# An RNN step with h stationary in four column tiles, and its sums turned on VectorE

## What is computed

```python
x = x + L0(x, cond)                       # modulated product with a 512x512 weight
# L1
xW = einsum('ntd,dh->nth', x, Wx) + b
h = cond
for t in range(128):
    h = tanh(h @ Wh + xW[:, t])           # 32x512 by 512x512
x = x + h_t
x = x + L2(x, cond)                       # base product and a low-rank one per sequence
x = x + L3(x, cond)                       # an LSTM over the 128 steps, 512 to 4x512
```

## Time and profile before

| | |
|---|---|
| median of 3 runs | 1167.6 us (1166.99 to 1167.61) |
| span of the profiled execution | 1166.8 us |
| mean granted clock of TensorE | 0.993 |
| TensorE busy | 1130.2 us (97%), 23548 matmuls |
| VectorE busy | 899.6 us (77%), 2660 instructions |
| ScalarE busy | 424.4 us (36%) |
| RNN matmuls | 2048 of 64 columns, 2048 of 32 columns |

### The profile page before, as it was taken

How to read it: one execution, slowest core, us unless ns; L and a number is a source line. 1 busy time by engine, 2 the same in 40 slices (tenths; PEclk the granted TensorE clock), 3 DMA queues, 4 the chain that set the end, 5 groups by cost and what they waited for, 6 DMA issues and landing times.

```text
span 1166.8 us, 52111 instructions
## 1 busy us (share of the span) xinstructions
PE 1130.2 (97%) x23548; PEld 773.9 (66%) x23548; DVE 899.6 (77%) x2660; ACT 424.4 (36%) x1036; POOL 53.7 (5%) x75
## 2 busy tenths in 40 slices
PE   5879999999999999999999999999999999999997
PEld 3546766776676677667667766766776676677587
DVE  6898877777877777787777778777777777777665
ACT  6784333333333333333333333333333333333232
POOL 1000100000000000000000000000000000000000
PEclk9889999999999999999999999999999999999999
DMA  9991000000000000000000000000000000000000
GB/s 337 404 347 33 21 21 21 3 21 21 21 20 21 21 3 21 21 21 21 21 20 4 21 21 21 21 21 17 7 21 21 21 21 21 12 3 12 12 13 21
DMA packets 24590, 51.08 MB, mean 44 GB/s; under 512 B 4160, under 2 KB 4288, under 8 KB 23344
## 3 DMA queue, kind: packets, MB, share of 16 engines
q1 hardware_dynamic: 23936, 47.49, 11.5%
q10 hardware_dynamic: 432, 0.26, 0.1%
HBM read 39.36 MB, written 8.39 MB: 41 GB/s over the span
## 4 chain that ended last, share of the span: by engine, by line
PE 92%; DMA 3%; DVE 2%; SPq 1%; ACT 1%; issue 1%; ACTq 0%; DVEq 0%
PE ps_gates L1523 55%; PE ps_l L1459 14%; PE ps_x L1459 7%; PE ps_rnn L1569 6%; PE ps_rnn L1572 4%; DMA ring<-in_hw 2%; PE ps_lr L1459 2%; PE ps_z L1459 2%; PE ps_l L1523 2%; SPq L395 1%; PE ps_gates L1429 1%; DMA rows<-in_ln_b 1%; SPq L426 0%; DVE gates_ring L1094 0%; SPq L415 0%
## 5 line engine op out<-in xcount | busy, mean ns | idle before, releaser
L1523 PE MATMUL ps_gates<-big,lstm_h 128*32 128x512 f16 (+1 forms) x6144 | 344.6, 373 | 1.5 <-DVE lstm_h L1127 1.2
L1523 PE MATMUL ps_gates<-big,rows 128*32 128x512 f16 (+1 forms) x6144 | 343.5, 372 | 0.6 <-ACT rows L514 0.6
L1523 PEld LDWEIGHTS ps_gates<-big,rows 128*32 128x32 f16 x6144 | 168.1, 97 | 158.8 <-issue 2.3
L1523 PEld LDWEIGHTS ps_gates<-big,lstm_h 128*32 128x32 f16 x6144 | 158.2, 97 | 148.1 <-DVE lstm_h L1127 2.0
L650 ACT ACTIVATE gates_ring<-gates_ring 128x256 f32<-128x256 f32 x128 | 53.4, 417 | 333.1 <-DVE gates_ring L1094 333.1
L1094 DVE SCALAR_TENSOR_TENSOR gates_ring<-ps_gates,tile_un,rows 128x256 f32<-128x256 f32 x248 | 108.6, 477 | 73.9 <-PE ps_gates L1523 73.9
L1569 PE MATMUL ps_rnn<-rnn_h,wh_hi 128*128 128x64 f16 x2048 | 120.5, 192 | 2.0 <-DVE rnn_h L928 1.9
L1572 PE MATMUL ps_rnn<-rnn_h,wh_lo 128*128 128x32 f16 x2048 | 116.3, 177 | 0.0
L1569 PEld LDWEIGHTS ps_rnn<-rnn_h,wh_hi 128*128 128x128 f16 x2048 | 93.0, 96 | 34.7 <-issue 27.4
L1572 PEld LDWEIGHTS ps_rnn<-rnn_h,wh_lo 128*128 128x128 f16 x2048 | 91.1, 97 | 0.0
L1124 DVE SCALAR_TENSOR_TENSOR late<-gates_ring,tile_g,cell_tanh 128x128 f16<-128x128 f32 x127 | 44.6, 352 | 60.2 <-ACT cell_tanh L659 60.2
(11 more groups left out here) (199 smaller groups left out, 1605.2 us busy)
## 6 DMA issues: line engine op xcount, KB each, us to landing
ring<-in_hw SPq DMA_DIRECT2D x16, 1024.0 KB, 14.8
xT_sb<-in_xT SPq DMA_DIRECT2D x32, 256.0 KB, 2.9
outT<-late SPq DMA_DIRECT2D x32, 256.0 KB, 2.0
big<-in_wx SPq DMA_DIRECT2D x5, 1024.0 KB, 14.7
big<-in_wh SPq DMA_DIRECT2D x5, 1024.0 KB, 14.3
big<-in_w SPq DMA_DIRECT2D x1, 1024.0 KB, 6.0
big<-in_hw SPq DMA_DIRECT2D x1, 1024.0 KB, 13.3
late<-in_base SPq DMA_DIRECT2D x1, 1024.0 KB, 14.3
```

Of the source, the lines that this page charges most:

```text
L1523: last = nc.tensor.matmul(by_chunk_of_gate(bank[B * j:B * j + B, columns]), of_step, tile_columns(w, j)[:, gates], start=start, stop=stop, ...
```

## The change

The two halves of the RNN weight become the two halves of one buffer, `wh1_16`. On TensorE h is stationary in four column tiles, as in the LSTM. The high half of h meets both halves of the weight in one matmul of 256 columns (128 of the high weight, 128 of the low); there are 16 of these (four chunks by four column tiles), and they wait for `rnn_hi_ready`. Then 16 matmuls of 128 columns take the low half of h with the high weight, behind the wait for `rnn_lo_ready`. So a step keeps 32 matmuls, streams 6144 columns where it streamed 1536, and does so in four tiles. The result, 128 partitions by 256 columns (two parts by four chunks by 32), has the batch on the partitions; VectorE turns its 32x32 blocks in one transpose from PSUM into a new buffer `rnn_turned` (fp32), and the two sums read that. The high and low half of h in `rnn_h16` lie one behind the other. The order of the steps in every engine's list is not changed.

```diff
--- before.py
+++ after.py
@@ -52,7 +52,8 @@
 
         w0_hi, w0_lo = sb("w0_hi", [P, KC, D], fp16), sb("w0_lo", [P, KC, D], fp16)
         wx1_hi, wx1_lo = sb("wx1_hi", [P, KC, H], fp16), sb("wx1_lo", [P, KC, H], fp16)
-        wh1_hi, wh1_lo = sb("wh1_hi", [P, KC, H], fp16), sb("wh1_lo", [P, KC, H], fp16)
+        wh1_16 = sb("wh1_16", [P, 2, KC, H], fp16)
+        wh1_hi, wh1_lo = wh1_16[:, 0], wh1_16[:, 1]
         base_hi, base_lo = sb("base_hi", [P, KC, D], fp16), sb("base_lo", [P, KC, D], fp16)
         a_hi, a_lo = sb("a_hi", [P, 2, KC, P], fp16), sb("a_lo", [P, 2, KC, P], fp16)
         b_hi, b_lo = sb("b_hi", [P, 2, D], fp16), sb("b_lo", [P, 2, D], fp16)
@@ -157,10 +158,11 @@
         b3_sb = rows[:, 0]
         x3_16 = [rows[:, 1 + q].bitcast(fp16).rearrange("p (h k n) -> p h k n", h=2, k=KC) for q in range(2)]
         x3_lr = rows[:, 3]
+        rnn_turned = sb("rnn_turned", [P, 2, KC, B])
         rnn_half = sb("rnn_half", [P, KC, B])
         rnn_pre = sb("rnn_pre", [P, KC, B])
         newton = sb("newton", [P, KC, B])
-        rnn_h16 = sb("rnn_h16", [P, KC, 2, B], fp16)
+        rnn_h16 = sb("rnn_h16", [P, 2, KC, B], fp16)
         cell = sb("cell", [P, P])
         added = sb("added", [P, P])
         cell_tanh = sb("cell_tanh", [P, P])
@@ -272,6 +274,7 @@
         x3_hi_ready, x3_lo_ready = sem("x3_hi_ready"), sem("x3_lo_ready")
 
         rnn_ps = sem("rnn_ps")
+        rnn_turned_ready = sem("rnn_turned_ready")
         rnn_half_ready = sem("rnn_half_ready")
         rnn_pre_ready = sem("rnn_pre_ready")
         rnn_h_ready = sem("rnn_h_ready")
@@ -304,6 +307,9 @@
 
         def tile_columns(w, j):
             return w.rearrange("p (k g j q) -> p j g k q", k=KC, g=GATES, q=B)[:, j]
+
+        def hidden_columns(w, j):
+            return w.rearrange("p h (k j q) -> p j h k q", j=KC, q=B)[:, j]
 
         def by_gate(x):
             return x.rearrange("p (g k q) -> p g k q", g=GATES, q=B)
@@ -638,7 +644,7 @@
 
             def rnn_high(r):
                 act.wait_ge(rnn_h_ready, r + 1)
-                high(rnn_h16[:, :, 0], x2T[r // STEPS % X2_RING][:, :, r % STEPS], s_h).then_inc(rnn_hi_ready, 1)
+                high(rnn_h16[:, 0], x2T[r // STEPS % X2_RING][:, :, r % STEPS], s_h).then_inc(rnn_hi_ready, 1)
 
             def rnn(r):
                 rnn_tanh(r)
@@ -693,7 +699,7 @@
             act.wait_ge(ld_wh1, 16)
             unused_squares(big[:, WH1_SLOT], 3, 2)
             act.wait_ge(h_scale_ready, 1)
-            high(rnn_h16[:, :, 0], condT_sb[:], s_h).then_inc(h0_hi, 1)
+            high(rnn_h16[:, 0], condT_sb[:], s_h).then_inc(h0_hi, 1)
             wx1_high(1)
             act.wait_ge(u_ready, 1)
             nc.scalar.activation(hyperT, hyperT, ACT.Gelu).then_inc(hyper_ready, 1)
@@ -915,17 +921,19 @@
                 dve.wait_ge(rnn_ps, r + 1)
                 if s == 0:
                     dve.wait_ge(xw1_ready, i + 1)
-                sums = ps_rnn[:, 0:2 * P].rearrange("p (k h b) -> p k h b", h=2, b=B)
-                nc.vector.scalar_tensor_tensor(rnn_half[:], sums[:, :, 1], un_rnn[:], xw1T[:, :, s],
+                nc.vector.transpose(rnn_turned[:].rearrange("p h k b -> p (h k) b"), by_chunk(ps_rnn[:, 0:2 * P]))\
+                  .then_inc(rnn_turned_ready, 1)
+                dve.wait_ge(rnn_turned_ready, r + 1)
+                nc.vector.scalar_tensor_tensor(rnn_half[:], rnn_turned[:, 1], un_rnn[:], xw1T[:, :, s],
                                                ALU.mult, ALU.add).then_inc(rnn_half_ready, 1)
                 dve.wait_ge(rnn_half_ready, r + 1)
-                nc.vector.scalar_tensor_tensor(rnn_pre[:], sums[:, :, 0], un_rnn[:], rnn_half[:],
+                nc.vector.scalar_tensor_tensor(rnn_pre[:], rnn_turned[:, 0], un_rnn[:], rnn_half[:],
                                                ALU.mult, ALU.add).then_inc(rnn_pre_ready, 1)
 
             def rnn_out(r):
                 i, s = r // STEPS, r % STEPS
                 dve.wait_ge(rnn_hi_ready, r + 1)
-                nc.vector.scalar_tensor_tensor(rnn_h16[:, :, 1], x2T[i % X2_RING][:, :, s], s_h, rnn_h16[:, :, 0],
+                nc.vector.scalar_tensor_tensor(rnn_h16[:, 1], x2T[i % X2_RING][:, :, s], s_h, rnn_h16[:, 0],
                                                ALU.mult, ALU.subtract).then_inc(rnn_lo_ready, 1)
 
             def x2(i):
@@ -1205,7 +1213,7 @@
                                     hb1T_sb[:].unsqueeze(2).broadcast_to([P, KC, B]), ALU.add).then_inc(u_ready, 1)
             wx1_low(0)
             dve.wait_ge(h0_hi, 1)
-            low(rnn_h16[:, :, 1], condT_sb[:], s_h, rnn_h16[:, :, 0]).then_inc(h0_lo, 1)
+            low(rnn_h16[:, 1], condT_sb[:], s_h, rnn_h16[:, 0]).then_inc(h0_lo, 1)
             weight_scale(3, 4, wh1_scale_ready)
             dve.wait_ge(wh1_scale_ready, 1)
             linked(nc.vector.tensor_tensor(un_rnn[:], s_wh1, s_h, ALU.mult))
@@ -1562,15 +1570,18 @@
                     gates_h(t, (1,), ((0, 0), (0, 1), (1, 0)), True).then_inc(gates_ps, 1)
 
             def rnn(r):
+                wait(pe, rnn_hi_ready, r)
+                for k in range(KC):
+                    for j in range(KC):
+                        nc.tensor.matmul(ps_rnn[B * j:B * j + B, 0:2 * P].rearrange("p (h k q) -> p h k q", h=2, q=B),
+                                         rnn_h16[:, 0, k], hidden_columns(wh1_16[:, :, k], j), start=(k == 0), stop=False,
+                                         tile_position=(0, B * j))
                 wait(pe, rnn_lo_ready, r)
-                for oc in range(KC):
-                    at = 2 * B * oc
-                    for k in range(KC):
-                        nc.tensor.matmul(ps_rnn[:, at:at + 2 * B], wh1_hi[:, k, P * oc:P * oc + P],
-                                         rnn_h16[:, k].rearrange("p h b -> p (h b)"), start=(k == 0), stop=False)
-                    for k in range(KC):
-                        last = nc.tensor.matmul(ps_rnn[:, at:at + B], wh1_lo[:, k, P * oc:P * oc + P], rnn_h16[:, k, 0],
-                                                start=False, stop=(k == KC - 1))
+                for k in range(KC):
+                    for j in range(KC):
+                        last = nc.tensor.matmul(by_chunk(ps_rnn[B * j:B * j + B, 0:P]), rnn_h16[:, 1, k],
+                                                hidden_columns(wh1_16[:, 0:1, k], j)[:, 0], start=False,
+                                                stop=(k == KC - 1), tile_position=(0, B * j))
                 last.then_inc(rnn_ps, 1)
 
             pe.wait_ge(consts_ready, 2)
```

## The result

| | before | after |
|---|---|---|
| median | 1167.4 us (measured beside it) | 1171.9 us (1170.35 to 1175.08) |
| ratio | 1 | 1.0043 [1.003, 1.0055] |
| span of the profiled execution | 1166.8 us | 1169.2 us |
| RNN step on TensorE | 0.88 us | 0.67 us |
| one tile | 34.05 us (the loop's first 34.45) | 33.9 to 34.4 us (the loop's first two 35.4 and 34.9, its last 33.2), mean of the loop 34.16 |

A forecast was written before the change was run, and what follows sets the result against it. TensorE was taken to bound the long middle. From a span of 1166.8 us, -24.9 (TensorE), +2.9 (stall) and +0.5 (start) make -21.5; with 0.8 to the median, 1146.1 us, range 1140 to 1166.

The forecast's parts named there:

- its saving: TensorE's RNN step falls from 0.88 to 0.67 us: 0.86 a tile, 24.9 us over 29 tiles.
- The changes of tiling: TensorE's switches between full-array and column-tiled work: moved at no cost; two more a tile would be 5 us.
- the wait for the high half: TensorE's new wait for the high half of h before an RNN step: met early, adding no delay.
- Rivals 1 and 3: TensorE's floor holds for every matmul, 1163 to 1168 us, 17%; VectorE's transpose dear, 1183 at 0.80 us, 8%.
- rival 2: VectorE bound a little, collision staying or dearer transpose: 0.2 to 0.5 us more stall a tile, 1152 to 1161 us, 15%.
- what was booked: New TensorE stall at the high half of the LSTM's h: 0.1 us a tile, 2.9 us in all.
- I give back 0.4 us: On VectorE, x1's low half moves away from GpSimd's product and shortens, cutting the added time from +1.10 to +0.70.
- the sums are as long from SBUF: VectorE's RNN sums take 349 ns from SBUF against 351 from PSUM, so moving their operand costs nothing.
- the first thing that is late: The high half of the LSTM's h, which TensorE takes up 1.32 us after it is ready, comes out level.
- the prediction's own sum: At the LSTM's high half of h: 1.5 us to spare, less VectorE's 0.70 and TensorE's 0.86, gives -0.06.
- The start was booked at +0.5: Eight RNN steps before 100 us, where DMA and VectorE rule: +0.5 us, bounds -3 and +3.
- nothing in the trace goes below about 27.5 ns: Possible TensorE floor per matmul with weight load, the low part's upper bound: 0.44 us, where 0.23 was taken.

The follow-up runs named there:

- e1: The changed kernel without VectorE's transpose, the sums reading PSUM unturned, so its RNN values are not the reference's: 1143.57 us.
- e13: The changed kernel with the wait for the low half of h ahead of all matmuls of an RNN step: 1171.15 us.
- e2: The changed kernel with the transpose writing the free half of its own PSUM bank, where the two sums read it: 1151.18 us.
- e8: e2 with VectorE taking lstm_sums(t + 1) before rnn_sums(r + 1), and x1_low and rnn_out(r + 1) behind the LSTM step: 1162.33 us.
- e14: e8 with ScalarE's order turned as well, the LSTM gates of step t + 1 ahead of the RNN's tanh: 1145.21 us.
- e3: The changed kernel with GpSimd's product for L0 held back until VectorE's tile scales after the second LSTM step: 1160.28 us.
- e10: The changed kernel with the transpose made twice in each RNN step: 1218.72 us.

## Why the prediction was wrong

**What held.** The windows were read rightly for before: TensorE was the bound. The step on TensorE is 0.67 us and its saving 25.1 us for 24.9 (e1), of which 23.0 in the tiles that were counted. The changes of tiling cost 0.05 us a tile at most, and the wait for the high half nothing that can be told (e13). The transpose takes 0.44 us, with its link 0.48. Rivals 1 and 3 are out: 128 columns in four tiles go 0.055 us a group, and the transpose is far from 0.67 us. What came is rival 2's mechanism, VectorE as the bound with the collision staying, but larger: 0.85 us of stall a tile is 0.75 over what was booked, where the rival gave 0.2 to 0.5.

**What failed, by size.** The step "I give back 0.4 us". It followed the low half of x1 out of GpSimd's product, rightly (745 ns in the mean of the 32), and did not ask what moved in. GpSimd starts the product a nearly fixed time after it has spread the maximum of x (7.49 us before, 7.24 now), and VectorE's queue behind that maximum had become longer by the transposes; so the instruction beside it was now an RNN sum. That sum had read one tensor from PSUM, and the change itself gave it both from SBUF. The prediction even compared the two forms, 349 against 351 ns, and took this for "the sums are as long from SBUF"; that is true only while GpSimd is quiet. Instead of 0.4 us a tile given back, VectorE has 22.5 us of stretching where it had 16.5. e2 takes exactly this away, and 21.2 of the 27.5 us between e1 and the kernel after go with it.

**What failed, by place.** The prediction took the high half of the LSTM's h for the first thing that is late. 2.6 us ahead of it TensorE needs the PSUM bank. In the trace of before, VectorE's timeline has the instruction that frees it:

```profile
520.55 0.86 DVE L1094 SCALAR_TENSOR_TENSOR gates_ring<-ps_gates,tile_un,rows 128x256 f32<-128x256 f32 x2
```

The line has both halves of the bank's sums; the second ends at 521.41. TensorE was to take the bank up halfway through the 96 products of 519.73, at 519.73 + 2.60 = 522.33: 0.92 to spare, not 1.32. No wait showed there, so no view named it; the code's waits do. A tile with a mean collision (0.45 us for this tile's 0.83) has 1.30. By the prediction's own sum with its 0.4 given back, 1.30 - 0.70 - 0.86 = -0.26 us a tile; the measured stall with nothing stretched is 33.37 - 33.24 = 0.13 (e2). With the collision kept and grown to 22.5 / 32 = 0.70 us, VectorE's addition is 1.10 + 0.70 - 0.45 = 1.35, and 1.30 - 1.35 - 0.86 = -0.91; measured is 34.09 (the median tile) - 33.24 = 0.85. So the method carries, given the right point and the right duration, though this was worked out with the result in hand; the 0.1 us a tile that was booked had both wrong. One term of the sum is also wrong by its own rows: 1.32 to spare beside a collision of 1.57 is 1.32 + 1.57 - 1.17 = 1.72 beside a median one, not 1.5. With 1.72 the sum gives +0.16, no stall at all, so this slip lay on the side of the result and hid a little of the miss.

**Why the time came out as if nothing had been saved.** The path that now sets the tile runs from the bank through one `gates_x` (2.60 us), one LSTM step's products (2.89 until VectorE takes them up at 531.72) and then VectorE's queue from there to the end of the next `lstm_sums(t + 1)` (559.31 + 0.87 = 560.18, so 28.46). These make 33.95 us from 526.23 to 560.18; with the 0.05 until TensorE starts, that tile is 34.00. No RNN matmul is in them. TensorE's saving could not shorten it; that it came to within 0.1 us of the old tile, nothing in the two traces ties together.

**The rest.** The start was booked at +0.5: the first LSTM step of the loop begins at 99.73, where it began at 98.91, so +0.8. The first two tiles took 35.42 and 34.90 us (e1: 34.06 and 33.24), which the prediction had as ordinary ones. From the kernel e1 to the kernel after the spans differ by 27.5 us: 25.8 in the 29 tiles (990.60 against 964.78), 0.8 in the start and 0.8 behind the loop. Against the kernel before, the kernel after is 2.8 us longer in the tiles and 0.8 in the start, and 1.3 shorter behind the loop. The range left out both the case that came and its size: "0.2 to 0.5 us of stall a tile" was bounded by a dearer transpose, not by a stretched sum.

## What to carry to other kernels

When a layout change moves an operand from PSUM to SBUF, price the instruction beside a GpSimd operation and not by its quiet duration, and ask which instruction will stand beside that operation once the queue has shifted. Before an engine's saving is counted, list from the code every wait of that engine on the engine that gets the new work, the freeing of buffers first, and take the slack at each, since a wait that is met early stands in no view. And an order turned on one engine is to be turned on its feeder as well: the same turn cost 11 us against e2 with ScalarE left as it was (e8) and gained 6 with it (e14).

## What the runs showed of the hardware

- The stretching depends on where the operands are. Beside GpSimd's product of 1.28 us a sum with both tensors in SBUF went from 0.35 to as much as 1.46 us (L930), while the same sum with one of them in PSUM stayed at 349 to 352 ns, 56 times (e2). The Trainium skill, page "SBUF — State Buffer", section "SBUF: two separate sides", says that a VectorE operation with two SBUF inputs and a GpSimd one that reads SBUF exclude each other on a shared port pair for the whole instruction. The trace agrees on which operands are hit, and that one waits for the other's end: in the kernel after, the hit sum ended 0.15 us behind the product in all 28 tiles that have one, wherever it had begun, and in the kernel before the low half of x1 (512 columns) ended 0.55 us behind it in 26 of the 28. A sum of 0.35 us that began only behind the product would end 0.35 behind it, so some 0.2 us of it, an estimate from these two numbers, are not held up.
- It goes the other way too. In e2 the sum into x1T, with both tensors in SBUF, was already running at 679.25 when the product began at 679.56: it kept its 0.69 us, and the product took 1.53 instead of 1.28.
- Not the size decides: an instruction of 128x2 elements went from 0.17 to 1.17 us (e3), ending within 0.03 us of the product's end. It reads one tensor only, and no run here shows why it is hit.
- Four matmuls of 128 columns in four column tiles go every 0.055 us (16 in 520.08 - 519.86 = 0.22), 14 ns a matmul. The full-array ones of before took 27.5 ns in the mean; those of 64 columns went every 29 ns and those of 32 every 26, so the prediction's "nothing in the trace goes below about 27.5 ns" was read off the mean. The floor of about 25 ns that the prediction weighed, from the Trainium skill, page "TensorE: Matmul & The Clock Gate", section "Wait — 56ns, not 53.3ns?", fits the full-array ones and does not hold across column tiles.
- After three of seven waits of 1.9 to 2.1 us in e10 TensorE's granted clock fell to 0.50, and 48 products took 4.3 us instead of 2.6; after the other four it did not fall, and no run here shows what decides it.
- A transpose of 32x32 blocks over 256 fp32 columns takes 442 ns from PSUM to SBUF and 456 from PSUM to PSUM; over 128 columns in SBUF it takes 311.
